# Negated maxima written by the reduction itself, expert ranks from one difference, a shorter inverse root and one table of whole-number distances

## What is computed

```python
x = layernorm(x + attn0(x))   # 16 heads of 8 channels; scores / sqrt(8) - slope_h * |i - j|; softmax; slope_h = 2 ** (-8 h / 16)
x = layernorm(x + moe0(x))    # softmax gate over 8 experts, top 2, silu(x W1 + b1) * (x W3 + b3) @ W2, and a shared expert
x = layernorm(x + attn1(x))   # keys at fixed shifts (16 distinct below 256), softmax over them, sigmoid gate
x = layernorm(x + moe1(x))    # gate over 8 experts, top 2, one matrix per expert
```

## Time and profile before

| | us |
|---|---|
| median of 3 runs (1722.67 to 1727.79) | 1725.61 |
| profiled execution | 1721.39 |
| its span, first to last instruction | 1719.6 |
| TensorE matmul busy in it | 1465.4 (85%) |
| VectorE busy | 1297.0 (75%) |
| ScalarE busy | 913.0 (53%) |
| GpSimd busy | 882.3 (51%) |
| mean granted TensorE clock | 0.958 of full speed |

### The profile page before, as it was taken

How to read it: one execution, slowest core, us unless ns; L and a number is a source line. 1 busy time by engine, 2 the same in 40 slices (tenths; PEclk the granted TensorE clock), 3 DMA queues, 4 the chain that set the end, 5 groups by cost and what they waited for, 6 DMA issues and landing times.

```text
span 1719.6 us, 36166 instructions
## 1 busy us (share of the span) xinstructions
PE 1465.4 (85%) x12928; PEld 1134.0 (66%) x12928; DVE 1297.0 (75%) x3466; ACT 913.0 (53%) x1868; POOL 882.3 (51%) x772
## 2 busy tenths in 40 slices
PE   2799889999999999999999999999999999985534
PEld 1567666776777767777777767677777767664423
DVE  2466888888888888788888888888888888875552
ACT  1356555566655555566655555566565556563310
POOL 0013565555556665555556665555555655555532
PEclk8799999999999999999999999999999999998765
DMA  4223344444444434544444334444444334433330
GB/s 120 98 93 95 113 131 126 152 144 131 138 132 134 128 115 138 152 148 128 139 136 132 126 114 139 152 130 146 124 147 125 119 126 145 148 87 108 83 111 31
DMA packets 88983, 214.26 MB, mean 125 GB/s; under 512 B 10499, under 2 KB 67075, under 8 KB 67459
## 3 DMA queue, kind: packets, MB, share of 16 engines
q1 hardware_dynamic: 88804, 211.95, 40.9%
HBM read 185.97 MB, written 25.69 MB: 123 GB/s over the span
## 4 chain that ended last, share of the span: by engine, by line
PE 39%; DVE 24%; issue 18%; POOL 11%; ACT 3%; DMA 3%; SPq 1%; DVEq 0%; POOLq 0%; ACTq 0%
POOL wb L1059 8%; PE b L508 7%; PE bPV L529 6%; DVE mx L993 5%; PE bS L546 4%; PE b L567 4%; PE bTU L558 4%; PE bTU L559 3%; POOL prod L1068 2%; DVE wb L962 2%; DVE wb L911 2%; PE bS L549 2%; DVE mneg L1036 2%; DVE gat L975 1%; DVE wb L969 1%
## 5 line engine op out<-in xcount | busy, mean ns | idle before, releaser
L1059 POOL TENSOR_TENSOR wb<-wb 128x1024 f32<-128x1024 f32 x64 | 150.6, 2354 | 498.0 <-DVE wb L911 498.0
L993 DVE TENSOR_REDUCE mx<-bS 128x2 f32<-128x512 f32 x512 | 338.5, 683 | 57.2 <-PE bS L549 55.7
L1068 POOL TENSOR_TENSOR prod<-kC,qC 128x512 f32<-128x512 f32 x256 | 349.1, 1399 | 37.2 <-ACT kC L670 37.2
L701 ACT ACTIVATE P<-bTU 128x512 f32<-128x512 f32 x512 | 277.0, 607 | 106.0 <-PE bTU L481 79.1
L1093 POOL TENSOR_TENSOR h<-ub,gBcb 128x256 f32<-128x256 f32 x256 | 184.0, 730 | 188.1 <-DVE ub L1006 153.5
L546 PE MATMUL bS<-stack 96*128 96x256 bf16 x1024 | 217.8, 280 | 35.3 <-DVE mx L993 14.8
L478 PE MATMUL bTU<-stack 97*128 97x256 bf16 x1024 | 227.3, 275 | 5.5 <-ACT P L701 2.5
L481 PE MATMUL bTU<-dist,identh 128*128 128x128 f16 x1024 | 206.5, 220 | 0.0
L558 PE MATMUL bTU<-x1T,w 128*128 128x256 f32 x576 | 184.1, 402 | 24.6 <-DVE h L1006 24.6
L549 PE MATMUL bS<-dist,identh 128*128 128x128 f16 x1024 | 197.1, 223 | 0.0
L710 ACT ACTIVATE sil<-bTU,b 128x256 f32<-128x256 f32 x288 | 130.1, 475 | 104.6 <-PE bTU L559 56.4
(11 more groups left out here) (159 smaller groups left out, 2781.7 us busy)
## 6 DMA issues: line engine op xcount, KB each, us to landing
wb<-d_w SPq DMA_DIRECT2D x64, 1024.0 KB, 7.8
stack<-d_parts SPq DMA_DIRECT2D x192, 192.0 KB
gBcb<-d_cB SPq DMA_DIRECT2D x32, 1024.0 KB, 4.8
gDcb<-d_cD SPq DMA_DIRECT2D x32, 1024.0 KB, 4.7
d_parts<-parts SPq DMA_DIRECT2D x96, 128.0 KB, 5.2
d_w<-wT SPq DMA_DIRECT2D x32, 256.0 KB, 2.1
xT<-in_xT SPq DMA_DIRECT2D x32, 128.0 KB, 4.7
x<-in_x SPq DMA_DIRECT2D x32, 128.0 KB, 2.1
```

Of the source, the lines that this page charges most:

```text
L701: act_f(P[k % 8][:].rearrange("p a b -> p (a b)"), bTU[turn_bank("ST", k)][:], ACT.Exp).then_inc(actA2.done("exp", k), 1)
L993: v.tensor_reduce(mx[:, :, k], bS[k % 2][:].rearrange("p (a b) -> p a b", a=TT), op=ALU.max, axis=AX.X).then_inc(dveA1.done("max", k), 1)
L1059: tt_(pv[:, 8 * n:8 * n + 4, :], pv[:, 8 * n:8 * n + 4, :], pv[:, 8 * n + 4:8 * n + 8, :], ALU.add).then_inc(poolC2.done("add", n), 1)
L1068: tt_(prod[:, 2 * p:2 * p + 2, :], shifted(kC, p), qC[:].unsqueeze(1).to_broadcast([128, 2, T]), ALU.mult).then_inc(poolC1.done("prod", p), 1)
```

## The change

- **Maxima.** `A1.max` writes the negated maximum straight into `mneg` (bf16). `M.neg`, its semaphore and the f32 tile `mx` go; `M.mT` waits for the sixteenth maximum; the first maximum of a pass waits until the last transposes have read `mneg`.
- **Ranks.** VectorE takes the difference of all pairs once and compares it with a table `least`, which holds minus the smallest normal number where the other index is lower and 0 elsewhere. Greater, equal, tie product and sum go: six operations in place of eight.
- **Inverse roots.** The first guess has another constant, then come one step of three operations with other constants and one of four, in place of three of three. `nt` counts seven in place of nine.
- **Distances.** q is scaled by 1 / (sqrt(8) slope) per channel, and the exponential by the slope of its head (an immediate number). So all heads share one `dist`, whole numbers in f16 (128 x 128 in place of 128 x 16 x 2 x 128), and the far distances fill four rows of the stack's table, the other eight are 0. `A2.ST` adds `dist` once in every head. The scale of q is a column `qs0`, loaded by a DMA of its own, and the ScalarE copies L650 and L655 read it as an operand.

```diff
@@ -57,7 +63,7 @@
         G.rank C2.pv.4 G.weigh C2.pv.5 C2.pv.6 C2.pv.7 C2.add.0 A1.max.0 A1.max.1 C2.add.1 A1.max.2 C2.add.2 A3.rec
         B.wu.0 C2.gt A1.max.3 B.wu.1 A1.max.4 A3.num A1.max.5 A1.max.6 B.wu.2 A1.max.7 A1.max.8 C2.res A1.max.9
         B.wu.3 A1.max.10 B.wu.4 A1.max.11 A1.max.12 C1.mx B.wu.5 B.wu.6 A1.max.13 A1.max.14 C1.sum B.wu.7 A1.max.15
-        M.neg A3.res B.wu.8""",
+        A3.res B.wu.8""",
     "pool": """
         C2.add.0 C2.add.1 C1.prod.0 C1.prod.1 C1.prod.2 C1.prod.3 C1.prod.4 C1.prod.5 C1.prod.6 C1.prod.7 B.h.1
         B.h.2 B.h.3 A3.xbo B.h.4 D.xs.0 B.h.5 B.h.6 D.xs.1 B.h.7 D.xs.2 B.h.8 C2.xb D.xs.3""",
...
@@ -477,10 +483,7 @@
                             c = slice(kt * T + kt * 128, kt * T + kt * 128 + 128)
                             mm(o[:, q], stack[odd][0:ROW_M + 1, 1, h, kt * 128:kt * 128 + 128],
                                stack[odd][0:ROW_M + 1, 0, h, :], start=True, stop=False)
-                            last_part = h % 2 == 0
-                            i = mm(o[:, c], identh[:], dist[:, h, 0, :], start=False, stop=last_part)
-                            if not last_part:
-                                i = mm(o[:, c], identh[:], dist[:, h, 1, :], start=False, stop=True)
+                            i = mm(o[:, c], identh[:], dist[:], start=False, stop=True)
                         i.then_inc(peA2.done("ST", k), 1)
...
@@ -611,7 +614,7 @@
                     if what == "M.mT" and (e := r["M"]) is not None:
 
                         take(7, ("M", actM, "mT", 0), t)
-                        pe.wait_ge(dveM.sem, dveM.count(e, "neg"))
+                        pe.wait_ge(dveA1.sem, dveA1.count(e, "max", 15))
                         o = b7[:].bitcast(BF)
                         for tt in range(TT):
...
@@ -648,12 +651,12 @@
                         act.wait_ge(peA1.sem, peA1.count(e, "qk"))
                         act.wait_ge(dveA1.sem, dveA1.count(e - 1, "lo"))
                         act_f(qk[:, 0, :], b6[:, 0:T], ACT.Identity, bias=bqk0[:, 0:1],
-                              scale=q_scale).then_inc(actA1.done("q"), 1)
+                              scale=qs0[:, 0:1]).then_inc(actA1.done("q"), 1)
                         act_f(qk[:, 1, :], b6[:, T:2 * T], ACT.Identity, bias=bqk0[:, 1:2]).then_inc(actA1.done("k"), 1)
 
                         act.wait_ge(st_part[0], dma_count(e - 1))
                         act_f(parts[:, 0, 0, :], b6[:, 0:T], ACT.Identity, bias=bqk0[:, 0:1],
-                              scale=q_scale).then_inc(actA1.done("hi", 0), 1)
+                              scale=qs0[:, 0:1]).then_inc(actA1.done("hi", 0), 1)
                         act_f(parts[:, 1, 0, :], b6[:, T:2 * T], ACT.Identity,
                               bias=bqk0[:, 1:2]).then_inc(actA1.done("hi", 1), 1)
                     if what == "B.xT" and (e := r["B"]) is not None:
@@ -698,7 +701,8 @@
                             act.wait_ge(pePV.sem, pePV.count(e, "PV", (k - 8) // 4))
                         else:
                             act.wait_ge(pePV.sem, pePV.count(e - 1, "PV", (k + 8) // 4))
-                        act_f(P[k % 8][:].rearrange("p a b -> p (a b)"), bTU[turn_bank("ST", k)][:], ACT.Exp).then_inc(actA2.done("exp", k), 1)
+                        act_f(P[k % 8][:].rearrange("p a b -> p (a b)"), bTU[turn_bank("ST", k)][:], ACT.Exp,
+                              scale=SLOPES[head(k)]).then_inc(actA2.done("exp", k), 1)
                     if what == "B.ab" and (e := r["B"]) is not None:
                         x = expert(n)
...
@@ -805,19 +809,26 @@
                     dve.wait_ge(dveN.sem, dveN.count(e, "ve"))
                     v.tensor_scalar(ni, nv.bitcast(I32), 1, None, ALU.logical_shift_right).then_inc(dveN.done("sh"), 1)
                     dve.wait_ge(dveN.sem, dveN.count(e, "sh"))
-                    v.tensor_scalar(nr.bitcast(I32), ni, -1.0, float(0x5F3759DF), ALU.mult,
+                    v.tensor_scalar(nr.bitcast(I32), ni, -1.0, float(0x5F1FFFF9), ALU.mult,
                                     ALU.add).then_inc(dveN.done("mg"), 1)
-                for n in range(3):
-                    if n + 1 in parts:
-
-                        dve.wait_ge(dveN.sem, dveN.count(e, "nt", 3 * n - 1) if n else dveN.count(e, "mg"))
-                        v.tensor_tensor(ns, nr, nr, ALU.mult).then_inc(dveN.done("nt", 3 * n), 1)
-                        dve.wait_ge(dveN.sem, dveN.count(e, "nt", 3 * n))
-                        v.scalar_tensor_tensor(ns, ns, -0.5, nv, ALU.mult, ALU.mult).then_inc(dveN.done("nt", 3 * n + 1), 1)
-                        dve.wait_ge(dveN.sem, dveN.count(e, "nt", 3 * n + 1))
-                        v.scalar_tensor_tensor(nr, ns, 1.5, nr, ALU.add, ALU.mult).then_inc(dveN.done("nt", 3 * n + 2), 1)
+                if 1 in parts:
+                    dve.wait_ge(dveN.sem, dveN.count(e, "mg"))
+                    v.tensor_tensor(ns, nr, nr, ALU.mult).then_inc(dveN.done("nt", 0), 1)
+                    dve.wait_ge(dveN.sem, dveN.count(e, "nt", 0))
+                    v.scalar_tensor_tensor(ns, ns, -ROOT_A, nv, ALU.mult, ALU.mult).then_inc(dveN.done("nt", 1), 1)
+                    dve.wait_ge(dveN.sem, dveN.count(e, "nt", 1))
+                    v.scalar_tensor_tensor(nr, ns, ROOT_B, nr, ALU.add, ALU.mult).then_inc(dveN.done("nt", 2), 1)
+                if 2 in parts:
+                    dve.wait_ge(dveN.sem, dveN.count(e, "nt", 2))
+                    v.tensor_tensor(ns, nr, nr, ALU.mult).then_inc(dveN.done("nt", 3), 1)
+                    dve.wait_ge(dveN.sem, dveN.count(e, "nt", 3))
+                    v.tensor_tensor(ns, ns, nv, ALU.mult).then_inc(dveN.done("nt", 4), 1)
+                    dve.wait_ge(dveN.sem, dveN.count(e, "nt", 4))
+                    v.scalar_tensor_tensor(ns, ns, -ROOT_C, ns, ALU.add, ALU.mult).then_inc(dveN.done("nt", 5), 1)
+                    dve.wait_ge(dveN.sem, dveN.count(e, "nt", 5))
+                    v.scalar_tensor_tensor(nr, ns, ROOT_D, nr, ALU.add, ALU.mult).then_inc(dveN.done("nt", 6), 1)
                 if 3 in parts:
-                    dve.wait_ge(dveN.sem, dveN.count(e, "nt", 8))
+                    dve.wait_ge(dveN.sem, dveN.count(e, "nt", 6))
                     v.scalar_tensor_tensor(n_b[:, rows, :], n_mv[:, rows, :, 0], -1.0, nr, ALU.mult,
                                            ALU.mult).then_inc(dveN.done("nb"), 1)
 
@@ -836,18 +847,15 @@
                 lg = gL[:, m].rearrange("p s t x -> p (s t) x")
                 lj = lg.unsqueeze(2).to_broadcast([128, n * TT, E, E])
                 li = lg.unsqueeze(3).to_broadcast([128, n * TT, E, E])
-                o = [x[:, m].rearrange("p s (t i j) -> p (s t) i j", t=TT, i=E) for x in (ggt, geq)]
-                v.tensor_tensor(o[0], lj, li, ALU.is_gt).then_inc(dveG.done("gt"), 1)
+                o = [x[:, m].rearrange("p s (t i j) -> p (s t) i j", t=TT, i=E) for x in (ggt, gdf)]
+                v.tensor_tensor(o[1], lj, li, ALU.subtract).then_inc(dveG.done("dif"), 1)
                 dve.wait_ge(dveG.sem, dveG.count(e, "gmx"))
                 v.tensor_tensor(gdl[:, m], gL[:, m], gmx[:, m].unsqueeze(3).to_broadcast([128, n, TT, E]),
                                 ALU.subtract).then_inc(dveG.done("sub"), 1)
-                v.tensor_tensor(o[1], lj, li, ALU.is_equal).then_inc(dveG.done("eq"), 1)
-                dve.wait_ge(dveG.sem, dveG.count(e, "eq"))
-                v.tensor_tensor(geq[:, m], geq[:, m], tri[:].unsqueeze(1).to_broadcast([128, n, TT * E * E]),
-                                ALU.mult).then_inc(dveG.done("eqt"), 1)
-                dve.wait_ge(dveG.sem, dveG.count(e, "eqt"))
-                v.tensor_tensor(ggt[:, m], ggt[:, m], geq[:, m], ALU.add).then_inc(dveG.done("add"), 1)
-                dve.wait_ge(dveG.sem, dveG.count(e, "add"))
+                dve.wait_ge(dveG.sem, dveG.count(e, "dif"))
+                v.tensor_tensor(ggt[:, m], gdf[:, m], least[:].unsqueeze(1).to_broadcast([128, n, TT * E * E]),
+                                ALU.is_gt).then_inc(dveG.done("gt"), 1)
+                dve.wait_ge(dveG.sem, dveG.count(e, "gt"))
                 v.tensor_reduce(grank[:, m].rearrange("p s t x -> p (s t x)"),
                                 ggt[:, m].rearrange("p s (a j) -> p (s a) j", j=E), op=ALU.add,
                                 axis=AX.X).then_inc(dveG.done("rank"), 1)
@@ -989,9 +997,9 @@
                         k = n
                         dve.wait_ge(peA1.sem, peA1.count(e, "S", k))
                         if k == 0:
-                            dve.wait_ge(dveM.sem, dveM.count(e - 1, "neg"))
-                        v.tensor_reduce(mx[:, :, k], bS[k % 2][:].rearrange("p (a b) -> p a b", a=TT), op=ALU.max,
-                                        axis=AX.X).then_inc(dveA1.done("max", k), 1)
+                            dve.wait_ge(peM.sem, peM.count(e - 1, "mT"))
```

(47 more changed lines are left out.)

23 lines of the change are left out of this document (11 added, 12 removed).

## The result

| | before | after |
|---|---|---|
| median of the runs | 1725.61 us | 1658.08 us (1656.38 to 1659.97) |
| ratio, 95% interval | | 0.9615 [0.9601, 0.9629] |
| profiled execution, its span | 1721.4, 1719.6 us | 1658.7, 1656.7 us |
| common step (mark to mark) | 48.56 us | 46.44 us |
| 26 steps in the middle | 1261.5 us | 1209.1 us |

67.5 us went, in the profiled execution 62.7; its span fell by 62.9, of which 52.4 in the 26 steps, 4.0 ahead of them and 6.5 behind.

The account below looks back on a forecast made before the run. A repeating ring of waits across engines, not one full engine, was taken as the bound. 23 x 2.00 + 3 x 1.10 = 49.3, plus 7.8, made 57.1 us off 1725.6: 1668 us, range 1650 to 1692.

Parts of the forecast that it names:

- The ring: Repeating chain of waits between engines, 48.52 us a step; negation, roots and ranking were all said to lie on it.
- Nothing of size changes: Rival: another ring of nearly 48 us lies beneath, so the time stays 1720 to 1730 us; chance 0.02.
- the ranking hidden: Rival: something beside the ranking ends there instead, 0.90 us a step lost, 1691 us; chance 0.10.
- The negation: VectorE's separate negation waits behind GpSimd's SBUF use; removal gains 0.90 us a step, TensorE's idle time before L617.
- The maxima: Sixteen VectorE maxima a step, now negated and in bf16, were taken to cost 0 extra.
- The rival with 0.2 us each: Rival: negating maxima are slower; at 0.2 us each a step grows by 1.2 us, 1749 us; chance 0.04.
- Ranking and roots: VectorE: two ranking operations fewer gain 0.90 us a step, two root operations fewer gain 0.40 us.
- Weights late: Rival: second attention's weights DMA comes late, GpSimd's first sum holds the difference; 0.5 us a step, 1681 us; chance 0.14.
- Pointer scale and distances: Two ScalarE copies with scale from an array cost 0.20 us a step; 16 fewer TensorE matmuls count 0.
- The sum: 0.90 + 0.40 + 0.90 - 0.20 = 2.00 us a common step; 57.1 us in all.
- The three that end with an unheld negation: Three of the 26 middle steps, like the one at 494.93, were said to gain only 1.10 us each.
- The twelve passes at the ends: Passes outside the 26 steps: between 0 and 1.3 us gained each, taken at half, 7.8 us.

Follow-up runs that it names:

- neg_as_reduce: Kernel before, its separate negation kept but written as a negating reduction over an axis of length one: 1699.7 us, ratio 0.9844.
- max_alone: Kernel before with only the maxima written negated and the separate negation removed: 1701.5 us, ratio 0.9857.
- logits_first_psum: Changed kernel with second transpose and gate logits ahead of the attention's product, ScalarE's list to match, and one operand of the difference from PSUM: 1691.9 us.
- all_four: Changed kernel with scale folded into q weights, two VectorE sums as one reduction, logits ahead of the attention's product, difference operand from PSUM: 1659.9 us.
- logits_first: Changed kernel with the second transpose and gate logits ahead of the attention's product on TensorE, ScalarE's list to match: 1692.4 us, ratio 0.9804.
- dist_alone: Kernel before with only the whole-number distances: scale from an array in two ScalarE copies, 16 small matmuls less, factor in the exponential: 1728.1 us.
- prescaled_q: Changed kernel with the scale of q multiplied into the q weights at setup and an immediate 1 in the copies: 1658.1 us, ratio 0.9597.

## Why the prediction was right

**The ring.** The claim that negation, roots and ranking lie one behind another on it holds: alone they give 0.99, 0.40 and 0.89, the prediction had 0.90, 0.40 and 0.90. "Nothing of size changes" and "the ranking hidden" fall.

**The negation.** Right in mechanism, 0.09 low. The 0.90 was TensorE's idle time up to its modelled end; without a wait the next matmul starts 0.07 us before that end. neg_as_reduce shows that the wait beside GpSimd was all that the operation cost.

**The maxima.** The term was 0. Sixteen at 6 ns more are 0.1 us of VectorE a step, of which the ring shows nothing: max_alone has them and neg_as_reduce hasn't, and both steps are 47.57 us. The rival with 0.2 us each is out by a factor of thirty.

**Ranking and roots.** Durations and marks as forecast: 0.42 us an operation, 1.57 us to the next product, ten operations after `n_v`. What the prediction did not see is how near the end of this gain was. It named TensorE's way to the scores as what might come next; it is the gates' exponential on ScalarE, with 0.06 us left, and the two kernels that shortened the way further (logits_first_psum, all_four) gained nothing by it even at full clock.

**Weights late.** Not seen: VectorE waits 3.6 us in all for this DMA, as before, GpSimd's first sum ends 0.28 us ahead of the difference, where 0.27 was the margin, and the difference takes 0.42. Where the difference was moved forward by 0.75 us (logits_first), the wait that this rival described did come, 0.35 us. The place of the hazard was right.

**Pointer scale and distances.** 0.176 us measured against 0.20 (582 ns a copy by the rows, 563 in fact), on the ring as said (dist_alone +0.19, prescaled_q -0.17). The matmuls count 0.03 or less, against 0.

**The sum.** The step that failed is small: 2.00 us a step was forecast and 2.12 came. The 26 steps gave 52.4 and not 49.3. Paired one by one, the 23 of the common kind gave 48.0 for 46.0. The three that end with an unheld negation gave 4.4 for 3.3: without the wait two of them were only 0.47 us shorter than the others before, not 0.90, so 1.10 was too little for them. The twelve passes at the ends gave 10.4 and not 7.8, taken at half between two bounds for want of anything better. These 5.7 us, and the 4.8 from the profiled execution of after lying 0.6 above its median where that of before lay 4.2 below, are the 10 us of difference.

## What to carry to other kernels

An idle gap in front of a dependent instruction is worth the time by which the *next* resource is free, not the length of the wait; price a chain of small operations by starts, and look at the in-order queue of every engine that feeds the end of the chain, since the next bound stood 0.06 us behind this gain, on an engine with nothing to do with the edit. A reordering that brings results forward can cost more than it wins: here it went with the lower clock in 21 steps of 26 for 4, so compare the granted clock step by step before believing a gain. What a slow stretch costs depends on what waits behind it, between nothing and 1.3 us here. A scale that can be folded into weights costs nothing per step, but look at the whole time too: here the 4.7 us won in the steps didn't show in the median.
